# Result rows of the last mixture stage in two planes, the lower one read back ahead of the last expert's work

## What is computed

```
scores = xf @ Wr + br                       # 2048 x 8
_, top_idx = jax.lax.top_k(scores, 2)
mask = one_hot(top_idx, 8).sum(-2) > 0
router_weights = softmax(where(mask, scores, -inf))
h = gelu(xf @ W1[e] + b1[e]);  y = h @ W2[e] + b2[e]
out = x + sum over the token's two experts of router_weights * y
```

## Time and profile before

| | us |
|---|---|
| median of 3 runs | 494.76 (493.02 to 497.63) |
| the profiled execution | 491.26 |
| its span from first to last instruction | 489.3 |
| attention of the second layer | about 240 to 391 |
| between the stages | 391 to 400 |
| mixture of the second layer | 400 to 476 |
| end (load, add, store) | 476 to 489 |

### The profile page before, as it was taken

One profiled execution on the slowest core, in us unless ns is written; L12 is line 12 of the kernel. 1 busy time (PEld: TensorE's weight loads), 2 busy tenths in 40 slices (PEclk: granted clock), 3 DMA queues, 4 the chain that ended last, 5 costly groups with the idle time before them and its releaser, 6 DMA issues.

```text
span 489.3 us, 11162 instructions
## 1 busy us (share of the span) xinstructions
PE 455.3 (93%) x3313; PEld 390.3 (80%) x3313; DVE 366.4 (75%) x1232; ACT 233.2 (48%) x578; POOL 298.1 (61%) x378
## 2 busy tenths in 40 slices
PE   6569999999999799999879999999999879999996
PEld 6458888889987467676568888888889769999995
DVE  7787898989986343333488999999999867776754
ACT  3226666666654755555524343352443224554331
POOL 7535677779855347777533576776676544576661
PEclk9678999999999999999989999999999969999999
DMA  7229999920001213221461310000000122322017
GB/s 220 29 51 361 349 342 348 352 69 23 24 23 38 72 50 97 77 59 38 155 209 54 88 50 28 32 23 13 17 18 12 42 67 61 82 68 69 32 33 255
DMA packets 48972, 49.30 MB, mean 101 GB/s; under 512 B 12701, under 2 KB 34680, under 8 KB 48915
## 3 DMA queue, kind: packets, MB, share of 16 engines
q1 hardware_dynamic: 43419, 39.73, 26.5%
q0 software_dynamic: 4544, 8.44, 5.3%
q10 hardware_dynamic: 952, 0.43, 0.4%
HBM read 20.97 MB, written 28.35 MB: 101 GB/s over the span
## 4 chain that ended last, share of the span: by engine, by line
PE 70%; SPq 11%; DVE 5%; ACT 4%; issue 3%; POOL 3%; DMA 3%; POOLq 0%; ACTq 0%
PE ps L1945 9%; PE ps L1873 7%; PE ps L1920 7%; PE ps L1746 6%; PE ps L1926 6%; PE ps L1849 6%; SPq L392 4%; SPq L398 4%; PE ps L1825 3%; PE ps L1863 3%; PE ps L1875 3%; PE ps L1642 2%; PE ps L1956 2%; PE ps L1912 2%; POOL ys L618 2%
## 5 line engine op out<-in xcount | busy, mean ns | idle before, releaser
L618 POOL DMA_INDIRECT ys<-ysbs,backs x78 | 76.5, 980 | 62.5 <-issue 21.3
L580 POOL TENSOR_TENSOR pp<-pp,rden 128x1232 f32<-128x1232 f32 x15 | 33.7, 2249 | 33.7 <-DVE x L1312 29.1
L561 POOL TENSOR_TENSOR qr<-qsm,mhalf 128x16 f32<-128x16 f32 x16 | 47.2, 2952 | 7.2 <-DVE qsm L1002 7.1
L1500 DVE TENSOR_TENSOR big<-big,ps 128x256 f32<-128x256 f32 x39 | 16.4, 421 | 44.1 <-ACT big L835 44.1
L554 POOL DMA_INDIRECT rows<-pays,slots x32 | 33.6, 1050 | 24.2 <-DVE slots L1126 12.2
L589 POOL DMA_INDIRECT rows<-pays,slots x32 | 32.7, 1020 | 20.8 <-DVE slots L1334 10.0
L840 ACT ACTIVATE big<-big 128x512 f32<-128x512 f32 x39 | 24.6, 630 | 39.4 <-PE ps L1945 35.1
L1926 PE MATMUL ps<-xsT,wups 128*128 128x128 f32 x312 | 43.2, 284 | 0.0
L1505 DVE TENSOR_TENSOR big<-ps,b1T 128x512 f32<-128x512 f32 x39 | 27.0, 692 | 19.5 <-PE ps L1926 19.2
L1945 PE MATMUL ps<-w2b,big 128*128 (+1 forms) x312 | 41.1, 275 | 0.0
L1746 PEld LDWEIGHTS ps<-region_a,pp 128*128 128x128 f32 x320 | 37.3, 191 | 3.9 <-issue 3.3
(11 more groups left out here) (319 smaller groups left out, 1254.7 us busy)
## 6 DMA issues: line engine op xcount, KB each, us to landing
rows<-empty SPq DMA_DIRECT2D x68, 258.0 KB, 4.4
xs<-rows SPq DMA_DIRECT2D x78, 64.5 KB, 1.9
region_b<-in_L_ffn_W_dram SPq DMA_DIRECT2D x2, 1024.0 KB, 9.4
yb_all<-ys SPq DMA_DIRECT2D x16, 128.0 KB, 2.4
region_a<-in_L_ffn_W_dram SPq DMA_DIRECT2D x8, 256.0 KB, 3.7
w2b<-in_L_ffn_W_dram SPq DMA_DIRECT2D x8, 256.0 KB, 4.1
keys<-ys SPq DMA_DIRECT2D x8, 256.0 KB, 3.5
ys<-ysbs,backs POOLq DMA_INDIRECT x78
```

Source lines behind the costliest of these rows:

```text
L561: pool.tensor_tensor(qr[s], qsm[s], mhalf[:, 0:H], ALU.pow).then_inc(a["qr"], 1)
L580: pool.tensor_tensor(p3, p3, rden[s].unsqueeze(2).to_broadcast([P, H, KEYS]), ALU.mult).then_inc(a["norm"], 1)
L618: pool.indirect_dma_start(ys[l][:, :], bass.IndirectOffsetOnAxis(backs[:, j % XB:j % XB + 1], 0), ysb[j % YB], None, bounds_check=2 * T - ...
```

## The change

The rows of `ys` are split into two planes of 2048 rows: the lower plane takes the result of the expert with the lower number, the upper plane that of the other. `turn` compares the two chosen numbers, `result_rows` writes the last column of `pay` from `plane`, `swing` and `turned`; it takes the place of the copy from `dest`. Since expert 7 is never the lower one, the lower plane is complete once the experts 0 to 6 are done. `lower_rows` computes how many scatters that is, and SP then loads the lower plane (four transfers of 256 KB), while the upper plane is loaded at the old place (eight of 128 KB). DVE and PE add the lower part first. `turned_gates` swaps the gates of turned tokens. `gates` moves from job 2 to job 5 and SP's wait for it from job 12 to job 20, in both layers. The transpose of the bias rows and eight fillers move ahead of the last tile's rank, four fillers stay after the count instead of eight, and the ten fillers ahead of the end go.

```diff
@@ SP
-                    if j == XB:
-                        sp.wait_ge(m["gates"], m.count("gates", 6))
+                    if j == XB + E:
+                        sp.wait_ge(m["gates"], m.count("gates", (6, 9)[l]))
...
+                if l == 1:
+                    lower = [sp.value_load(need_lo[0:1, at(r)], min_val=80, max_val=512) for r in range(YB)]
+                    for r in range(YB):
+                        sp.wait_ge(sentb[r], lower[r])
+                    for b in range(NBATCH):
+                        sp.dma_start(ylast[:, 0, b * TPB:(b + 1) * TPB, :].rearrange("p t d -> p (t d)"), ylo_v[b]).then_inc(pro1[f"ylo{b}"], 16)
                 for r in range(YB):
                     sp.wait_ge(sentb[r], landed[r])
...
-                sp.dma_start(ylast[n].rearrange("p t k d -> p (t k d)"), ylast_v[n // 2, n % 2]).then_inc(xs_in[n], 16)
+                sp.dma_start(ylast[:, 1, 2 * n:2 * n + 2, :].rearrange("p t d -> p (t d)"), yhi_v[n // 2, n % 2]).then_inc(pro1[f"yhi{n}"], 16)
@@ POOL
+            pool.memset(swing[:, 0:1], float(T))
+            pool.memset(swing[:, 1:2], -float(T))
...
+            def result_planes():
+                pool.iota(planei[:, :, :].rearrange("p (b t) k -> p b t k", b=NBATCH), [[SEQ, NBATCH], [1, TPB], [T, 2]], base=0, channel_multiplier=TPB).then_inc(const, 1)
+                pool.wait_ge(const, NCONST + 1)
+                pool.tensor_copy(plane[:, :, :], planei[:, :, :]).then_inc(const, 1)
...
+                    if l == 0 and i == 12:
+                        result_planes()
@@ ACT
-                    n, k = (j - 6) // 2, (j - 6) % 2
+                    n, k = (j - 14) // 2, (j - 14) % 2
...
+                if l == 1:
+                    act.wait_ge(pro1["b1T"], pro1.count("b1T", 1))
+                    act.copy(b1T[:, :, :], TP[0][:, 0:E * F1 // P].rearrange("p (e k) -> p e k", e=E)).then_inc(pro1["b1Ts"], 1)
                 act.wait_ge(M[l]["margin"], M[l].count("margin", 2 - l))
@@ DVE
+            def turn(t):
+                dve.tensor_tensor(turned[:, t:t + 1], topi[t % 2][:, 0:1], topi[t % 2][:, 1:2], ALU.is_gt).then_inc(A[1]["turn"], 1)
+
+            def result_rows(t):
+                if t == 0:
+                    dve.wait_ge(const, NCONST + 2)
+                dve.wait_ge(A[1]["turn"], A[1].count("turn", t + 1))
+                dve.scalar_tensor_tensor(pay[t % PB][:, :, D:ROW].bitcast(I32), swing[:, :].unsqueeze(2), turned[:, t:t + 1],
+                                         plane[:, t, :].unsqueeze(2), ALU.mult, ALU.add)
...
-                    if j == 2:
+                    if j == 5:
                         gates(l)
+                    if l == 1 and j == 8:
+                        lower_rows()
+                    if l == 1 and j == 11:
+                        turned_gates()
@@ DVE, end
             for n in range(NT // 2):
                 t = 2 * n
-                dve.wait_ge(xs_in[n], 16 * (2 * ring_uses(n, XB) + 1))
...
+                dve.wait_ge(pro1[f"ylo{t // TPB}"], pro1.count(f"ylo{t // TPB}", 16))
+                dve.scalar_tensor_tensor(ylast[:, 0, t, :], ylast[:, 0, t, :], gate[:, 0, t:t + 1], x[:, t, :], ALU.mult, ALU.add).then_inc(m["fin0"], 1)
+            for n in range(NT // 2):
+                t = 2 * n
                 dve.wait_ge(m["fin0"], m.count("fin0", n + 1))
+                dve.wait_ge(pro1[f"yhi{n}"], pro1.count(f"yhi{n}", 16))
+                dve.scalar_tensor_tensor(x[:, t, :], ylast[:, 1, t, :], gate[:, 1, t:t + 1], ylast[:, 0, t, :], ALU.mult, ALU.add).then_inc(m["fin"], 1)
@@ PE
+                    if l == 1 and i == NT + 6:
+                        pe.wait_ge(ld["moe1"], WEIGHTS1)
+                        tr(TP[0][:, 0:E * F1 // P], b1rows[:, :], ident[0:E * F1 // P, 0:E * F1 // P]).then_inc(pro1["b1T"], 1)
+                        keep_busy(8, TP[1])
...
-                    keep_busy(8, TP[1])
+                    keep_busy(4, TP[1])
...
-            keep_busy(10, MA)
```

More of the change, by code:

```diff
@@ L301, in bass_xattn_moe_two_layers @@
         PRO1 = ["fv", "foldT", "fT", "vals1", "b1T", "b1Ts", "diag", "mix", "mixed"]
+        PRO1 += [f"ylo{b}" for b in range(NBATCH)] + [f"yhi{n}" for n in range(NT // 2)]
         STATS = ["bnA", "mvA", "veA", "rsA"]
@@ L812, in moe @@
                 m = M[l]
-                if l == 1:
-                    act.wait_ge(pro1["b1T"], pro1.count("b1T", 1))
-                    act.copy(b1T[:, :, :], TP[0][:, 0:E * F1 // P].rearrange("p (e k) -> p e k", e=E)).then_inc(pro1["b1Ts"], 1)
                 for j in range(NJ + 2):
@@ L1261, in drain1 @@
                 if t < NT:
+                    if t == NT - 4:
+                        result_rows(t)
                     place(a, t)
@@ L1270, in drain1 @@
                     choose(a, t, scr[s])
+                    turn(t)
                     if t == NT - 1:
@@ L1273, in drain1 @@
                     payload(1, t)
-                    dve.tensor_copy(pay[t % PB][:, :, D:ROW].bitcast(I32), dest[:, t, :].unsqueeze(2))
+                    result_rows(t)
                 t = i - 4
@@ L1414, in step1 @@
                                       topi[s][:, 0:2].unsqueeze(2).to_broadcast([P, 2, E]), ALU.is_equal).then_inc(a["oh"], 1)
+                if 0 <= i - 5 < NT:
+                    turn(i - 5)
                 t = i + 1
@@ L1473, in gates, with lower_rows, turned_gates @@
                 dve.scalar_tensor_tensor(need[l][:, :], need_n[:, :], 16.0, need_base[:, l, :], ALU.mult, ALU.add).then_inc(m["gates"], 1)
+            def lower_rows():
+                m = M[1]
+                dve.tensor_tensor(real[:, :], jidx_all[:, :], cum[:, E - 2:E - 1].to_broadcast([1, NJR]), ALU.is_lt).then_inc(m["gates"], 1)
+                dve.wait_ge(m["gates"], m.count("gates", 7))
+                dve.reduce_sum(need_n[:, :], real[:, :].rearrange("a (u k) -> a k u", k=YB), AX).then_inc(m["gates"], 1)
+                dve.wait_ge(m["gates"], m.count("gates", 8))
+                dve.scalar_tensor_tensor(need_lo[:, :], need_n[:, :], 16.0, need_base[:, 1, :], ALU.mult, ALU.add).then_inc(m["gates"], 1)
+            def turned_gates():
+                m = M[1]
+                dve.wait_ge(m["gates"], m.count("gates", 3))
+                dve.tensor_tensor(gtmp[:, 1, :], gate[:, 1, :], gate[:, 0, :], ALU.subtract).then_inc(m["gates"], 1)
+                dve.wait_ge(m["gates"], m.count("gates", 10))
+                dve.tensor_tensor(gtmp[:, 0, :], gtmp[:, 1, :], turned[:, :], ALU.mult).then_inc(m["gates"], 1)
+                dve.wait_ge(m["gates"], m.count("gates", 11))
+                dve.tensor_tensor(gate[:, 0, :], gate[:, 0, :], gtmp[:, 0, :], ALU.add)
+                dve.tensor_tensor(gate[:, 1, :], gate[:, 1, :], gtmp[:, 0, :], ALU.subtract).then_inc(m["gates"], 1)
             expert = []
```

43 lines of the change are left out of this document (22 added, 21 removed).

## The result

The changed kernel takes 488.07 us (median of 4 runs, 487.6 to 488.27), the kernel before 494.5 us (4 runs, 493.02 to 497.63). The ratio is 0.9866, with a 95% interval of 0.9835 to 0.9897: 1.3% faster. The profiled execution of the changed kernel took 487.96 us, with a span of 486.1 us, where before had 491.26 and 489.3. So the medians differ by 6.4 us and the two traces by 3.2. Half of what follows is about that difference.

The account below looks back on a forecast made before the run. Four successive stretches bound it: PE-full attention, fillers at low clock between stages, PE-bound jobs, SP's end. Terms -4.4 - 3.2 + 0.2 + 0.1 = -7.3 us from 494.76 give 487.5; own range 486 to 489.5, overall 484.5 to 492.0.

Parts of the forecast that it names:

- The base of the sum: Whole kernel: -7.3 us taken from the one trace of before, span to 482.0, profiled execution 491.26 to 484.0.
- the constant of 3.5 us: Whole kernel: median of three runs lies 3.5 us above the profiled execution, so 494.76 - 7.3 = 487.5.
- Part 1: Between the stages: fillers and bias transpose ahead of the last rank keep the clock high; -4.4 us, bounds -3.0 to -5.0.
- the 1.6 us from job 0's bias to the first down: Start of the jobs: bias 0.69, gelu 0.63 and three hand-overs make 1.6 us, first down at 400.5.
- Rival (a): Between the stages: clock falls all the same, behind the fillers; gain there -2.1, total -5.0, 489.8 us; chance 0.12.
- Part 2: End of the kernel: lower plane loaded early, half-size upper loads, last store at 483.8 instead of 487.05; -3.2, bounds -2.2 to -3.9.
- the landing: End of the kernel: last upper load issued by 479.1 lands 2.6 us later, by 481.7; after that nothing waits for loads.
- SP's row of stores: End of the kernel: chain is SP's stores, seven steps of 0.46 us, as PE needs only 0.24 per pair.
- Part 3: Attention tiles, DVE: `turn` and `result_rows` added, a copy removed; +0.2 us over all tiles, bound above +5.3.
- (c): Attention tiles: `result_rows` pays by itself, about 0.3 us in 13 tiles, +3.9; total -3.6, 491.2 us; chance 0.07.
- (d): End: lower plane isn't early, twelve loads in a row, end gains 0.3; total -4.4, 490.4 us; chance 0.03.
- (e): Jobs: clock falls and stays low for two ten-microsecond stays, +10.2; total +2.9, 497.7 us, slower; chance 0.05.

Follow-up runs that it names:

- the control: Changed kernel unaltered, run again in the third session on chip 12: ratio 0.9903 to the kernel before.
- before again: Kernel before, unaltered, run again in the second session for a second trace: ratio 1.0025.
- after again: Changed kernel unaltered, run again in the first session for a second trace: ratio 0.9867 to the kernel before.
- The experiment with the copy first: Changed kernel with ScalarE's gelu one round later, behind the copy of the next job's transposed rows: ratio 0.9915 to the kernel before.
- the two experiments: Changed kernel with bias transpose and copy back behind the count, early fillers kept: 0.9892; changed kernel without the eight early fillers, third session: 0.9901.
- the planes alone: Changed kernel with eight fillers and bias transpose back in their old places; planes, early loading, turn and result rows kept: ratio 0.9973 to the kernel before.
- The two experiments with a second queue: Changed kernel with odd pairs' stores on ACT's queue: ratio 0.9907; with four upper loads and four stores on ACT's queue: 0.9948.

## Why the prediction was right, and where it wasn't

The forecast of 487.5 us and a gain of 7.3 stands beside 488.07 and 6.4 by the medians. Like for like, the first trace of before and the control, both without the stop, give 9.46 - 13.05 = -3.6, 0.0 in the jobs and 12.58 - 15.6 = -3.0, with +0.2 in the attention: -6.4. With the stop, before again and after again: -2.6, 0.0 and -3.0, +0.4: -5.2. Neither pair is a check on the times. The timed runs give 6.4 us at first, 6.6 in the first session and 4.8 in the control's, with intervals that overlap; the forecast's 7.3 lies inside the first two intervals (up to 8.2 and 8.7 us) and outside the third (up to 6.3). No trace of before was taken in the control's session.

**The base of the sum.** The span was to be 482.0 and the profiled execution 484.0; they were 486.1 and 487.96. This is the step that came out worst. I took the profiled execution as a fair sample and added its distance of 3.5 us to the median as a constant. It lacks the stop of 1.8 us, which the trace after has, as do the eight traces of the first two sessions, kernel before included. It goes with the session, or with its chip, and not with the version. So the pair of first traces hides 1.8 us of the change. Another 1.1 us is the end of that one trace, 13.64 where the control has 12.58: 0.4 of it is the landing of the last real scatter (SP's loads start 2.56 us behind the scatter's start, 2.18 in the control), the rest the stores. That the median came within 0.6 us of the forecast all the same is in part luck, since the constant of 3.5 us rests on a single execution. The bounds of the parts, added up, reach to 489.9 (-3.0 - 2.2 + 0.3), not 489.5. What makes the stop is open.

**Part 1** (-4.4, bounds -3.0 to -5.0): -3.5 in the pair of first traces and -3.6 in the control. The mechanism was right: the clock stays high, fillers take 0.13 each, the bias columns are early. The size was off in one term, the 1.6 us from job 0's bias to the first down. It is 2.72 to 2.76 us in every trace with ACT's old order but the first of before, where it is 3.05: bias 0.69, gelu 0.63, then the copy of the next rows, transpose and eight up matmuls, which the code puts ahead of the first down. I had counted hand-overs alone, and the row of up matmuls on PE was 0.9 us that the rows didn't hide. The experiment with the copy first took 0.93 us of it away at that place.

What within the part did the work was also not as the prediction had it. I wrote that the bias transpose and the fillers together free the path. By the two experiments the transpose's place is worth nothing once the clock is high (9.45 against 9.46), the early fillers 1.3 us (10.73 against 9.46). The rest, 12.75 to 13.05 down to 10.73, comes without the early fillers: four fillers fewer behind the count, eight instructions at 0.235, are 1.9 us at the low level, and the low stretch is shorter. The chains bear it out: sixteen late filler instructions stand in it with 3.62 us in the first trace of before, eight with 1.92 us in the second trace without early fillers. Late fillers alone were not varied in a run.

**Rival (a)**, the clock falls all the same, happened in part: three of the nine traces with early fillers show a fall, for 3.4 us and not for ten, at a cost of 0.6 to 1.0 us against the control and not 2.3. The six others show none (9.4 to 9.6 us, and 10.36 in one where job 0's bias waits for matmuls that by the profile had long ended). All five traces without early fillers show one, of 6.8 or 10.2 us. So the fall does come out differently from one execution to the next, which was the condition I gave it; the Trainium skill (TensorE: Matmul & The Clock Gate, section "What's actually happening"), with its free-running window, says the same, and these traces agree as to that.

**Part 2** (-3.2, bounds -2.2 to -3.9): the end is 12.3 to 13.6 us in the eight traces that have this end unaltered, 12.8 in the mean, against 15.6 to 15.9: -2.9. Right in size, and near the named places: the lower loads go out 5.1 us ahead of the last real scatter in the control (468.74 and 473.86; 3.4 in the trace after) where the sum put them 5.4 ahead, and the first store leaves 4.7 to 4.8 us behind the first upper load in both, as in the sum. The stores, 4.40 us, wait for ACT and DVE for 1.5 us in all, where before's waited 4.6. But the sum had nothing wait for a load any more. The trace after shows otherwise: the third upper load is in only 4.67 us after its issue, in the chain of waits

```profile
475.84 4.67 DMA keys<-ys
480.51 0.04 issue
480.56 2.21 PE ps L2065 x12
```

and twelve matmuls wait for it, six pairs at once. The term that was off is the landing, which I took as 2.6 us, the least that the rows show: 3.6 to 4.4 in this trace, 2.1 to 3.6 in the control. From the first store to the last it is 4.0 us here and 3.5 in the control instead of 3.2. In other traces it lies otherwise: with the planes alone every upper load lands in 2.5 to 2.6 us, and the end still takes 13.33. That the chain at the end would be SP's row of stores was not confirmed, and not refuted either: the profile's chain goes by the loads and ends with ACT's last copy, without any store, and SP starts its last store 0.7 us behind that copy in the trace after and 2.3 us with the planes alone. The two experiments with a second queue, written from that picture, gained nothing.

**Part 3** (+0.2): right in size, and partly by luck. From the first scores of the last attention stage to its last, 117.86 us before and 118.10 in the control: +0.24. It isn't spread over all tiles, as I had it: 0.2 of it is one tile, whose scores come 9.0 us behind the last ones where the other full tiles keep 8.82, as before the change. In the trace after, POOL's instruction starts 0.3 us late in that tile, and `result_rows` is held for 0.73 us instead of 0.41:

```profile
332.32 2.25 POOL L600 TENSOR_TENSOR pp<-pp,rden 128x1232 f32<-128x1232 f32 x1 [1.73 <-DVE x L1349]
333.86 0.73 DVE L1261 SCALAR_TENSOR_TENSOR pays<-swing,turned,plane 128x2 int32<-128x2 f32 x1
```

Why POOL starts late there is open. In the other full tiles `result_rows` is held together with the instruction behind it, and 0.33 + 0.15 stand where 0.41 stood. The rule of the Trainium skill (SBUF — State Buffer, section "SBUF: two separate sides") that I had weighed agrees: the first of the two DVE instructions ends 0.02 us after POOL's, takes 0.32 to 0.73 us beside it and 0.21 to 0.22 without it. **Rivals (c), (d) and (e)** did not come: no 0.3 us per tile, lower loads early, and in no trace a low stretch between the first down and the last real scatter.

## What to carry to other kernels

A sum that is made against one trace has the errors of two: of the steps, and of what that execution happened to have or lack. Compare stretches between named instructions, in more than one trace of each version, before a difference of two spans is given to the change. And where work is moved off a path at a low clock, recompute what ends last with the clock restored: here DVE's schedule took PE's place, so moving the bias transpose as well bought nothing.

## What was not expected of the hardware

In nine traces of two versions and their variants, the completion of a row of TensorE matmuls in the jobs reached ACT and DVE late, in the trace after 2.5 us behind its end by the profile, once per execution, fourteen or fifteen jobs behind the first down; in five others, at the same place, not at all (70.25 to 70.78 us against 68.70). It goes by the session in which they ran, eight traces on chip 3 with it and four on chip 12 without, not by the kernel; session and chip can't be told apart. The profile models the ends of matmuls, so late matmuls would look the same as late signals. What delays them, and whether it happens without the profiler, is open. The kernel before takes 496.6 and 496.7 us in the two sessions with the stop and 492.55 in the one without, which is more than 1.8 us apart.

At the same place the clock was at the low level for nothing or 3.4 us with the early fillers (nine traces), for 6.8 us with neither early nor more than four late ones (two) and for 10.2 us with eight late ones alone (three). The unaltered changed kernel did both: nothing twice, 3.4 us once.

ACT's DMA queue, whose list has six register loads and six waits ahead of the loads, started them 2.15 us behind SP's, which had the registers ready. That it is these loads that take the time was not run by itself.
